# A recurrent scan beside a mixture of experts: VectorE's gate and GpSimd's expert product change places, the convolution leaves VectorE

## The chip, the core and the metric

The kernel runs on one core of a Trainium2 chip. The metric is the device time of one execution in microseconds. Five engines work beside one another, each through its own list of instructions in order: TensorE (PE in the rows; its weight loads are PEld), VectorE (DVE), ScalarE (ACT), GpSimd (POOL) and SyncE (SP), which only starts transfers. They wait for one another by semaphores alone.

## What is computed

For 4096 tokens of width 256, after a layer norm:

```
left, right = split(layernorm(xn) @ W_up + b_up)           # 128 + 128 channels
left  = silu(conv(left, 3 taps) + conv_b)                  # causal, per channel
delta = softplus(left @ W_delta + b_delta);  B, C = left @ W_B, left @ W_C
h[t]  = exp(delta[t] * A) * h[t-1] + delta[t] * left[t] * B[t]   # 128 channels x 64 states
y[t]  = sum over states of h[t] * C[t]  + left[t] * D
s     = xn + (y * silu(right)) @ W_down + b_down
g     = silu(sum over the 2 best of 8 experts of weight * (silu(xn @ w1) * (xn @ w3)) @ w2)
out   = x + s * g
```

## The kernel before

**The recurrence** has 128 x 64 rows of 4096 steps. Time is cut into 8 chunks of 512 steps, and each chunk into 64 *pairs* (two channels by 64 states on the 128 partitions), 512 pairs in all, numbered s. For each pair TensorE spreads delta*left over the partitions (`spread`, L1236), VectorE multiplies it by B (`mult`, L955), ScalarE forms exp(delta*A) (L733), VectorE scans (`scan`, L964), GpSimd multiplies by C (`state_by_c`, L433), and TensorE adds four pairs at a time into y (`reduce_quad`, L1170). The product of `mult` goes to a ring of two slots (B_RING), so `mult(s)` waits until `scan(s-2)` is through.

**The experts** are worked on between the pairs. There are 71 places for tiles of 128 rows, of which 67 are live with this data; from pair 16 on a tile takes 7 pairs, from tile 67 on 5. A tile has four steps, in its pairs 0, 2, 4 and 5: TensorE makes both products (L1222) in one of two banks, ScalarE takes tanh (L662, into th) and copies the other half (L664, into ue), VectorE gates (L976: th and the bank give gt), GpSimd multiplies gt by ue (`hidden`, L448), and TensorE applies w2 (`expert_out`, L1192) in pairs 3, 6, 8 and 8 of the tile. The rows of the next tile are transposed in pair 6 (L1205), and ScalarE evicts them (L654). A bank is taken again two turns later, and TensorE then waits for the gate that read it. The turns of a pair stand in `BY_PAIR[s]`.

**The order on each engine** is that of the loops over s, written by hand. TensorE in turn s issues `spread(s+1)`, a quad every fourth pair, and then the turns of pair s. VectorE: `mult(s)`, `scan(s-1)`, `gates` of pair s-1. GpSimd: `state_by_c(s-1)`, then `after_turns` of pair s-1 (`hidden`, or the gather of the next rows), then the scatter of results. ScalarE: the exp of pair s, then the work of the pair, then the evictions of pair s.

**The work for the next chunk** is spread over the pairs by a table, `WORK_AFTER`, with the number of parts in `WORK_PARTS`: the convolution on VectorE in pairs 14 to 16 of a chunk (L991 for the first tap, L994 for the two others), both tanhs on ScalarE in pair 17 (L600, L601), both sums with 1 in pair 18 (L606, L607), the two products on GpSimd in 19 and 20 (L475, L481), and later the softplus. Chunk 0 is prepared before the loop, its convolution on TensorE.

**The end**: after the pairs, the two results of each token are added (L542), passed through the silu, and mixed with x. The eight loads of x for this (L386, 512 KB each) are issued on SyncE's queue in one row in pair 12 of the last chunk, where the same queue also carries the expert weights and, for a tile that keeps its expert, the release of the next tile's weight slots (L350).

## Time and profile before

| | us |
|---|---|
| median of 3 runs (lowest, highest) | 1382.23 (1381.26, 1382.64) |
| the profiled execution: device time | 1385.34 |
| the profiled execution: its span | 1382.9 |

| engine | busy us | share of the span |
|---|---|---|
| TensorE | 1205.3 | 87% |
| VectorE | 1193.4 | 86% |
| GpSimd | 1089.5 | 79% |
| ScalarE | 734.1 | 53% |

The span goes from the first to the last instruction of the profiled execution; its device time holds 2.4 us more, and is 3.1 us above the median. The loop over pairs lies between about 113 and 1345 us, and the live expert tiles between about 183 and 1285 us. Where two starts on one engine are subtracted, the difference is called a pitch: VectorE starts an instruction before the last one has ended by its record, so that a pitch can be shorter than the duration.

### The profile page before, as it was taken

How to read it: one execution, taken by the hardware profiler on the slowest of the kernel's cores; microseconds unless marked ns; L12 is line 12 of the kernel's file. 1: busy time of each engine (PE TensorE's matmuls, PEld its weight loads, DVE VectorE, ACT ScalarE, POOL GpSimd, SP SyncE). 2: the span in 40 equal slices, each digit the busy share in tenths (PEclk: the TensorE clock that was granted, in tenths of full speed). 3: DMA queues.
4: the chain of work that ended last, by engine and by line, in shares of the span. 5: the costliest groups of instructions: out<-in, count | busy, mean ns of one | idle time of the engine just before them, and what ended most of it. 6: DMA issues, size and time to landing. Idle time of an engine off the chain costs nothing.

```text
span 1382.9 us, 26003 instructions
## 1 busy us (share of the span) xinstructions
PE 1205.3 (87%) x7688; PEld 938.9 (68%) x7688; DVE 1193.4 (86%) x1634; ACT 734.1 (53%) x1583; POOL 1089.5 (79%) x1048
## 2 busy tenths in 40 slices
PE   4846788999999999998899989998999999989761
PEld 4725366877677777876687768686777777877530
DVE  6747588999799998989798979898989988988988
ACT  1361556555655565546554565456545565545642
POOL 0346278898899788888998788788979788988994
PEclk8579999999999999999999999999999999999655
DMA  7111264646364645564556436643664457464458
GB/s 211 61 39 46 67 212 135 168 141 214 110 175 143 198 148 165 147 212 121 148 147 211 126 119 180 214 142 103 172 211 139 127 155 230 143 222 149 144 175 291
DMA packets 124316, 216.51 MB, mean 157 GB/s; under 512 B 15040, under 2 KB 40768, under 8 KB 124160
## 3 DMA queue, kind: packets, MB, share of 16 engines
q10 hardware_dynamic: 73728, 134.25, 33.9%
q1 hardware_dynamic: 43616, 61.83, 13.6%
q0 software_dynamic: 6816, 18.62, 4.2%
q8 instruction: 65, 1.06, 0.3%
q14 instruction: 91, 0.75, 0.2%
HBM read 190.67 MB, written 23.99 MB: 155 GB/s over the span
## 4 chain that ended last, share of the span: by engine, by line
PE 68%; POOL 9%; issue 8%; DVE 6%; DMA 4%; ACT 3%; SPq 1%; ACTq 0%; DVEq 0%; POOLq 0%
PE bank L1222 31%; PE bank L1192 14%; PE bank L1170 8%; PE bank L1236 6%; POOL arena L433 4%; DMA wring<-in_w_all 3%; PE bank L1099 2%; POOL hid L448 2%; DVE arena L964 2%; PE bank L1115 1%; PE bank L1135 1%; PE bank L1068 1%; PE bank L1061 1%; SPq L386 1%; PE bank L1205 1%
## 5 line engine op out<-in xcount | busy, mean ns | idle before, releaser
L433 POOL TENSOR_TENSOR arena<-arena,c_rep 128x512 f32<-128x512 f32 x512 | 607.1, 1190 | 153.4 <-DVE arena L964 145.6
L964 DVE TENSOR_TENSOR_SCAN arena<-bank,carry,arena 128x512 f32<-128x512 f32 x512 | 652.5, 1275 | 30.7 <-ACT bank L733 30.5
L1222 PEld LDWEIGHTS bank<-xgT,wring 128*128 128x128 f32 x4288 | 518.3, 194 | 138.4 <-issue 99.3
L1222 PE MATMUL bank<-xgT,wring 128*128 128x128 f32 x4288 | 540.6, 280 | 50.5 <-issue 26.4
L733 ACT ACTIVATE bank<-arena,a_neg 128x512 f32<-128x512 f32 x512 | 354.2, 692 | 107.7 <-ACT bank L733 43.2
L955 DVE TENSOR_TENSOR arena<-bank,b_rep 128x512 f32<-128x512 f32 x512 | 351.8, 687 | 42.6 <-PE bank L1236 23.4
L662 ACT ACTIVATE th<-bank 128x256 f32<-128x256 f32 x284 | 108.9, 383 | 347.0 <-PE bank L1222 324.9
L1236 PE MATMUL bank<-stack,pick 128*128 128x512 f32 x512 | 279.1, 546 | 8.3 <-DVE arena L955 7.9
L1192 PE MATMUL bank<-wring,hid 128*128 128x256 f32 x1072 | 271.4, 386 | 8.2 <-POOL hid L448 7.4
L1192 PEld LDWEIGHTS bank<-wring,hid 128*128 128x128 f32 x1072 | 196.1, 191 | 64.4 <-issue 24.6
L448 POOL TENSOR_TENSOR hid<-gt,ue 128x256 f32<-128x256 f32 x284 | 209.6, 738 | 15.4 <-DVE gt L976 11.8
L976 DVE SCALAR_TENSOR_TENSOR gt<-th,bank 128x256 f32<-128x256 f32 x284 | 114.9, 404 | 63.7 <-ACT th L662 47.9
L1170 PE MATMUL bank<-arena,win 128*32 128x512 f32 x1024 | 143.3, 633 | 7.7 <-POOL arena L433 7.6
L1236 PEld LDWEIGHTS bank<-stack,pick 128*128 128x128 f32 x512 | 101.5, 198 | 27.4 <-DVE arena L955 12.1
L664 ACT ACTIVATE ue<-bank 128x256 f32<-128x256 f32 x284 | 107.3, 378 | 0.0
L453 POOL DMA_INDIRECT results<-o_sb,dest x71 | 72.8, 1025 | 12.9 <-issue 12.3
L423 POOL DMA_INDIRECT xg<-xn_d,source x71 | 70.9, 998 | 10.7 <-issue 3.8
L1170 PEld LDWEIGHTS bank<-arena,win 128*32 128x32 f32 x1024 | 20.6, 110 | 50.9 <-issue 35.1
L407 POOL TENSOR_SCALAR pick<-hid,mask 128x2048 fp32r<-128x2048 f32 x2 | 10.9, 5468 | 45.6 <-DVE mask L813 45.6
L672 ACT ACTIVATE o_sb<-bank,weight 128x256 f32<-128x256 f32 x71 | 32.7, 460 | 10.1 <-PE bank L1192 10.1
L1061 PE MATMUL bank<-ident,xn 128*128 128x128 f32 x64 | 15.2, 421 | 18.4 <-DVE xn L804 18.4
L1157 PEld LDWEIGHTS bank<-ident 128*128 128x128 f32 x72 | 18.4, 310 | 18.7 <-issue 17.9
(172 smaller groups left out, 818.9 us busy)
## 6 DMA issues: line engine op xcount, KB each, us to landing
arena<-delta_d ACTq DMA_DIRECT2D x512, 256.0 KB
wring<-in_w_all SPq DMA_DIRECT2D x64, 384.0 KB, 5.6
xn<-in_x SPq DMA_DIRECT2D x4, 1024.0 KB, 9.9
xn_d<-xn SPq DMA_DIRECT2D x4, 1024.0 KB, 5.5
parts_d<-spare SPq DMA_DIRECT2D x16, 256.0 KB
stack<-parts_d SPq DMA_DIRECT2D x16, 256.0 KB, 5.7
wring<-results SPq DMA_DIRECT2D x8, 512.0 KB, 7.3
arena<-results SPq DMA_DIRECT2D x8, 512.0 KB, 7.9
```

What stands on the lines that cost most here:

```text
L433: pool.tensor_tensor(p_ring[:, s % P_RING, :], h_ring[:, s % H_RING, :], of_chunk(c_rep, c, 2), ALU.mult).then_inc(s_hc, 1)
L448: pool.tensor_tensor(hid[:, k % 4, :], gt[:, k % 2, :], ue[:, k % 2, :], ALU.mult).then_inc(s_hid, 1)
L662: act.activation(th[:, :], bank[:, 0:SW], ACT.Tanh, scale=0.5).then_inc(s_th, 1)
L664: act.activation(ue[:, k % 2, :], bank[:, SW:2 * SW], ACT.Copy).then_inc(s_ue, 1)
L733: act.activation(a_bank[s % 2][:, :], dl_ring[:, s % D_RING, :], ACT.Exp, scale=a_neg[:, s % PAIRS:s % PAIRS + 1]).then_inc(s_exp, 1)
L955: v.tensor_tensor(b_ring[:, s % B_RING, :], du_bank[s % 2][:, :], b_rep[:, cols(c)], ALU.mult).then_inc(s_bm, 1)
L964: v.tensor_tensor_scan(out=h_ring[:, s % H_RING, :], data0=a_bank[s % 2][:, :], data1=b_ring[:, s % B_RING, :], initial=carry[:, q:q + 1], ...
L976: v.scalar_tensor_tensor(out=gt[:, k % 2, :], in0=th[:, :], scalar=1.0, in1=bank_of((turn, i, j))[:, 0:SW], op0=ALU.add, op1=ALU.mult).the ...
L1170: ins = pe.matmul(y_bank[32 * g:32 * g + 32, :], win[:, 30 - 2 * i:62 - 2 * i], p_ring[:, (4 * q + g) % P_RING, :], start=False, stop=(i = ...
L1192: ins = pe.matmul(o_bank[:, 0:D], hid[:, k % 4, m * SLOT:(m + 1) * SLOT], wring[:, 2 * r + m, 4 * P:WROW], start=(r == 0 and m == 0), stop ...
L1222: ins = pe.matmul(bank[:, m * SW + r * SLOT:m * SW + (r + 1) * SLOT], wring[:, 2 * j + r, (2 * m + h) * P:(2 * m + h + 1) * P], xgT[:, i % ...
L1236: pe.matmul(du_bank[s % 2][:, :], pick[:, QUADS * (g % 2) + i16, :], stack[:, c % 2, g // 2, :], start=True, stop=True).then_inc(s_sel, 1)
```

## The change

VectorE's turn becomes `mult(s)`, `gates` of pair s-2, `scan(s-1)`. GpSimd's turn becomes `after_turns` of pair s-2, `state_by_c(s-1)`. The convolution is made by three ScalarE instructions (each tap's product, in pairs 10 to 12) and two GpSimd additions (pairs 12 and 13); the tanhs and the sums with 1 are taken one a pair, in pairs 15 to 18. The eight loads of x start in pair 10 of the last chunk, one every fifth pair.

VectorE, pairs 301 to 304, without other work between: L955 is the multiply, L964 the scan (its form is printed as SCALAR_TENSOR_TENSOR), L976 the gate.

```order
L955 TENSOR_TENSOR arena<-bank,b_rep 128x512
L964 SCALAR_TENSOR_TENSOR arena<-bank,carry,arena 128x512
L976 SCALAR_TENSOR_TENSOR gt<-th,bank 128x256
L955 TENSOR_TENSOR arena<-bank,b_rep 128x512
L964 SCALAR_TENSOR_TENSOR arena<-bank,carry,arena 128x512
L976 SCALAR_TENSOR_TENSOR gt<-th,bank 128x256
L955 TENSOR_TENSOR arena<-bank,b_rep 128x512
L964 SCALAR_TENSOR_TENSOR arena<-bank,carry,arena 128x512
L955 TENSOR_TENSOR arena<-bank,b_rep 128x512
```

The same place after; the multiply is L986 there, the scan L995 and the gate L1007.

```order
L986 TENSOR_TENSOR arena<-bank,b_rep 128x512
L995 SCALAR_TENSOR_TENSOR arena<-bank,carry,arena 128x512
L986 TENSOR_TENSOR arena<-bank,b_rep 128x512
L1007 SCALAR_TENSOR_TENSOR gt<-th,bank 128x256
L995 SCALAR_TENSOR_TENSOR arena<-bank,carry,arena 128x512
L986 TENSOR_TENSOR arena<-bank,b_rep 128x512
L1007 SCALAR_TENSOR_TENSOR gt<-th,bank 128x256
L995 SCALAR_TENSOR_TENSOR arena<-bank,carry,arena 128x512
L986 TENSOR_TENSOR arena<-bank,b_rep 128x512
L995 SCALAR_TENSOR_TENSOR arena<-bank,carry,arena 128x512
```

Both gates have moved from behind a scan to between a multiply and a scan, and every multiply now stands directly behind a scan.

VectorE, pairs 398 to 400, where the convolution of the last chunk stands (L991, L994; L1002 adds the output product).

```order
L955 TENSOR_TENSOR arena<-bank,b_rep 128x512
L964 SCALAR_TENSOR_TENSOR arena<-bank,carry,arena 128x512
L1002 TENSOR_TENSOR xn<-xn,bank 128x512
L991 TENSOR_SCALAR spare<-c_rep,half 128x512
L955 TENSOR_TENSOR arena<-bank,b_rep 128x512
L964 SCALAR_TENSOR_TENSOR arena<-bank,carry,arena 128x512
L976 SCALAR_TENSOR_TENSOR gt<-th,bank 128x256
L994 SCALAR_TENSOR_TENSOR spare<-c_rep,half,spare 128x512
L955 TENSOR_TENSOR arena<-bank,b_rep 128x512
L964 SCALAR_TENSOR_TENSOR arena<-bank,carry,arena 128x512
L976 SCALAR_TENSOR_TENSOR gt<-th,bank 128x256
L994 SCALAR_TENSOR_TENSOR spare<-c_rep,half,spare 128x512
```

The same place after.

```order
L986 TENSOR_TENSOR arena<-bank,b_rep 128x512
L1007 SCALAR_TENSOR_TENSOR gt<-th,bank 128x256
L995 SCALAR_TENSOR_TENSOR arena<-bank,carry,arena 128x512
L1021 TENSOR_TENSOR xn<-xn,bank 128x512
L986 TENSOR_TENSOR arena<-bank,b_rep 128x512
L995 SCALAR_TENSOR_TENSOR arena<-bank,carry,arena 128x512
L986 TENSOR_TENSOR arena<-bank,b_rep 128x512
L1007 SCALAR_TENSOR_TENSOR gt<-th,bank 128x256
L995 SCALAR_TENSOR_TENSOR arena<-bank,carry,arena 128x512
L986 TENSOR_TENSOR arena<-bank,b_rep 128x512
```

The three instructions of the convolution are gone from VectorE; nothing takes their place.

GpSimd in the pairs around 394: L433 is the product by C, L448 the expert product, L423 and L453 are the gather and the scatter.

```order
L448 TENSOR_TENSOR hid<-gt,ue 128x256
L433 TENSOR_TENSOR arena<-arena,c_rep 128x512
L423 DMA xg<-xn_d,source 128x256
L433 TENSOR_TENSOR arena<-arena,c_rep 128x512
L448 TENSOR_TENSOR hid<-gt,ue 128x256
L433 TENSOR_TENSOR arena<-arena,c_rep 128x512 x2
L448 TENSOR_TENSOR hid<-gt,ue 128x256
L453 DMA results<-o_sb,dest 17280x256
```

The same place after; L436 is the product by C, L451 the expert product, L478 the new addition.

```order
L451 TENSOR_TENSOR hid<-gt,ue 128x256
L436 TENSOR_TENSOR arena<-arena,c_rep 128x512
L426 DMA xg<-xn_d,source 128x256
L436 TENSOR_TENSOR arena<-arena,c_rep 128x512
L451 TENSOR_TENSOR hid<-gt,ue 128x256
L436 TENSOR_TENSOR arena<-arena,c_rep 128x512
L478 TENSOR_TENSOR spare<-spare 128x512
L436 TENSOR_TENSOR arena<-arena,c_rep 128x512
L456 DMA results<-o_sb,dest 17280x256
L478 TENSOR_TENSOR spare<-spare 128x512
L451 TENSOR_TENSOR hid<-gt,ue 128x256
```

The expert products stand ahead of the products by C of their turn, and two additions have come in.

```diff
-WORK_AFTER = dict(conv=("pairs", 14), tanh=("pairs", 17), sigmoid=("pairs", 18), silu=("pairs", 19), right=("pairs", 20),
+WORK_AFTER = dict(conv=("pairs", 10), add=("pairs", 12), tanh=("pairs", 15), sigmoid=("pairs", 17), silu=("pairs", 19),
...
+AGAIN_AT = (NC - 1) * PAIRS + 10
...
-                if s == (NC - 1) * PAIRS + 12:
+                if s == AGAIN_AT:
...
-                    for c in range(NC):
-                        sp.dma_start(x_again[c], x[0, cols(c), :].rearrange("(n p) c -> p n c", p=P)).then_inc(s_again, 16)
+                if s >= AGAIN_AT and (s - AGAIN_AT) % 5 == 0 and s < AGAIN_AT + 5 * NC:
+                    c = (s - AGAIN_AT) // 5
+                    sp.dma_start(x_again[c], x[0, cols(c), :].rearrange("(n p) c -> p n c", p=P)).then_inc(s_again, 16)
...
+            def add_taps(c, part):
+
+                pool.wait_ge(s_taps, 3 * (c - 1) + part + 2)
+                if part:
+                    pool.wait_ge(s_first_sum, c)
+                pool.tensor_tensor(stage("cv"), stage("cv"), stage(("thl", "thr")[part]), ALU.add
+                                   ).then_inc(s_cvs if part else s_first_sum, 1)
...
+                if s > 1:
+                    after_turns(BY_PAIR[s - 2])
                 if s:
                     state_by_c(s - 1)
-                    after_turns(BY_PAIR[s - 1])
...
+            def tap_product(c, part):
+
+                if part == 0:
+                    act.wait_ge(s_partd, STORES * c)
+                    act.wait_ge(s_lrev, c + 1)
+                tap = 2 - part
+                act.activation(stage(("cv", "thl", "thr")[part]), of_chunk(c_rep, c, tap), ACT.Identity,
+                               bias=0.0 if part else half[:, 3:4], scale=half[:, tap:tap + 1]).then_inc(s_taps, 1)
...
                 mult(s)
+                if s > 1:
+                    gates(BY_PAIR[s - 2])
                 if s:
                     scan(s - 1)
-                    gates(BY_PAIR[s - 1])
...
-                for name, t, r in WORK[s]:
-                    if name == "conv":
-                        conv(t, r)
+            gates(BY_PAIR[PAIR_COUNT - 2])
             scan(PAIR_COUNT - 1)
```

## Rows read from the trace of the kernel before

**Rows 1.** The page's first part: busy us, share of the span, instructions of an engine.

```profile
PE 1205.3 (87%) x7688; PEld 938.9 (68%) x7688; DVE 1193.4 (86%) x1634; ACT 734.1 (53%) x1583; POOL 1089.5 (79%) x1048
```

**Rows 2.** The timeline of pairs 302 to 304: start us, us, engine, line, operation.

```profile
854.18 0.69 DVE L955 TENSOR_TENSOR arena<-bank,b_rep 128x512 f32<-128x512 f32 x1
...
854.78 1.28 DVE L964 TENSOR_TENSOR_SCAN arena<-bank,carry,arena 128x512 f32<-128x512 f32 x1
...
854.94 0.35 PEld L1205 LDWEIGHTS bank<-ident,xg 128*128 128x128 f32 x2
...
855.12 0.38 ACT L662 ACTIVATE th<-bank 128x256 f32<-128x256 f32 x1 [0.57 <-PE bank L1222]
...
855.75 0.69 ACT L733 ACTIVATE bank<-arena,a_neg 128x512 f32<-128x512 f32 x1
855.98 0.40 DVE L976 SCALAR_TENSOR_TENSOR gt<-th,bank 128x256 f32<-128x256 f32 x1
...
856.14 1.09 POOL L433 TENSOR_TENSOR arena<-arena,c_rep 128x512 f32<-128x512 f32 x1 [0.42 <-DVE arena L964]
856.29 0.69 DVE L955 TENSOR_TENSOR arena<-bank,b_rep 128x512 f32<-128x512 f32 x1
...
856.89 1.27 DVE L964 TENSOR_TENSOR_SCAN arena<-bank,carry,arena 128x512 f32<-128x512 f32 x1
...
857.19 0.73 POOL L448 TENSOR_TENSOR hid<-gt,ue 128x256 f32<-128x256 f32 x1
857.55 1.86 PEld L1222 LDWEIGHTS bank<-xgT,wring 128*128 128x128 f32 x16 [0.84 <-issue]
...
858.27 0.69 DVE L955 TENSOR_TENSOR arena<-bank,b_rep 128x512 f32<-128x512 f32 x1
```

**Rows 3.** VectorE's busy time in the seven pairs from 296 on, by stretch.

```profile
841.64:856.29 14.65, 14.27 (x20) 1.00 0.60 169
```

**Rows 4.** The timeline: VectorE's multiplies of pairs 16 and 485.

```profile
184.24 0.68 DVE L955 TENSOR_TENSOR arena<-bank,b_rep 128x512 f32<-128x512 f32 x1
...
1284.62 0.68 DVE L955 TENSOR_TENSOR arena<-bank,b_rep 128x512 f32<-128x512 f32 x1
```

**Rows 5.** The page's costliest groups: count, busy us, mean ns, idle us before and releasers.

```profile
L976 DVE SCALAR_TENSOR_TENSOR gt<-th,bank 128x256 f32<-128x256 f32 x284 | 114.9, 404 | 63.7 <-ACT th L662 47.9
```

**Rows 6.** Groups by line: the convolution, one GpSimd product and one ScalarE sum.

```profile
L994 DVE SCALAR_TENSOR_TENSOR spare<-c_rep,half,spare 128x512 f32<-128x512 f32 x14 | 19.2, 1374 | 0.0
...
L475 POOL TENSOR_TENSOR spare<-spare 128x512 f32<-128x512 f32 x8 | 10.2, 1275 | 20.7 <-ACT spare L607 20.7
...
L991 DVE TENSOR_SCALAR spare<-c_rep,half 128x512 f32<-128x512 f32 x7 | 8.1, 1157 | 0.0
...
L607 ACT ACTIVATE spare<-spare 128x512 f32<-128x512 f32 x8 | 4.9, 617 | 0.0
```

**Rows 7.** The timeline behind the convolution's second instruction in pair 399.

```profile
1086.83 1.48 DVE L994 SCALAR_TENSOR_TENSOR spare<-c_rep,half,spare 128x512 f32<-128x512 f32 x1
...
1088.23 0.68 DVE L955 TENSOR_TENSOR arena<-bank,b_rep 128x512 f32<-128x512 f32 x1
...
1090.46 1.86 PEld L1222 LDWEIGHTS bank<-xgT,wring 128*128 128x128 f32 x16 [1.32 <-DVE gt L976]
```

**Rows 8.** The timeline in pair 464: SyncE's last load of x, TensorE's next step.

```profile
1237.05 4.49 SPq L386 DMA_DIRECT2D c_rep<-in_x  x1
...
1242.12 2.71 PE L1222 MATMUL bank<-xgT,wring 128*128 128x128 f32 x16 [4.00 <-SPq L350]
```

**Rows 9.** The timeline late in the loop: two multiplies with a gate between.

```profile
1321.43 0.69 DVE L955 TENSOR_TENSOR arena<-bank,b_rep 128x512 f32<-128x512 f32 x1
...
1323.54 0.69 DVE L955 TENSOR_TENSOR arena<-bank,b_rep 128x512 f32<-128x512 f32 x1
```

More of the change, by code:

```diff
@@ L42 @@
 LOAD_OF = dict(step=4, out=2, rows=1, down=2, delta=2, b=2, c=2)
-WORK_AFTER = dict(conv=("pairs", 14), tanh=("pairs", 17), sigmoid=("pairs", 18), silu=("pairs", 19), right=("pairs", 20),
+WORK_AFTER = dict(conv=("pairs", 10), add=("pairs", 12), tanh=("pairs", 15), sigmoid=("pairs", 17), silu=("pairs", 19),
+                  right=("pairs", 20),
                   exp=("delta", 2), ln=("delta", 3),
@@ L47 @@
                   stack=("delta", 17))
-WORK_PARTS = dict(sum=4, conv=3)
+WORK_PARTS = dict(sum=4, conv=3, add=2, tanh=2, sigmoid=2)
 BIAS_AT = 61
+AGAIN_AT = (NC - 1) * PAIRS + 10
 def turns_by_pair():
@@ L264, in mamba_and_experts @@
         s_val, s_hot, s_perm, s_placed = (sem(k) for k in ("s_val", "s_hot", "s_perm", "s_placed"))
-        s_cv, s_cvs, s_taps, s_tanh, s_sig, s_u, s_sr = (sem(k) for k in ("s_cv", "s_cvs", "s_taps", "s_tanh", "s_sig", "s_u", "s_sr"))
+        s_cv, s_cvs, s_taps, s_first_sum, s_tanh, s_sig, s_u, s_sr = (sem(k) for k in ("s_cv", "s_cvs", "s_taps", "s_first_sum", "s_tanh", "s_sig", "s_u", "s_sr"))
         s_dp, s_bc, s_bcev, s_sp, s_dlt, s_hi = (sem(k) for k in ("s_dp", "s_bc", "s_bcev", "s_sp", "s_dlt", "s_hi"))
@@ L477, in gate_of_right @@
             def gate_of_right(c):
-                pool.wait_ge(s_sig, c + 1)
+                pool.wait_ge(s_sig, 2 * c + 2)
                 ge(pool, s_dn, 2 * (c - 1))
@@ L525, in _ @@
                 for name, c, r in WORK[s]:
-                    if name == "silu":
+                    if name == "add":
+                        add_taps(c, r)
+                    elif name == "silu":
                         silu_of_left(c)
@@ L535, in _ @@
                     bias_rows(s // PAIRS)
+            for here in BY_PAIR[PAIR_COUNT - 2:PAIR_COUNT]:
+                after_turns(here)
             state_by_c(PAIR_COUNT - 1)
@@ L595, in evict_conv, with tanhs, sigmoids @@
                 act.activation(stage("cv"), product_bank(c, "conv")[:, :], ACT.Identity, bias=half[:, 3:4]).then_inc(s_cvs, 1)
-            def tanhs(c):
-                act.wait_ge(s_cvs, c + 1)
-                act.activation(stage("thl"), stage("cv"), ACT.Tanh)
-                act.activation(stage("thr"), b_rep[:, cols(c)], ACT.Tanh).then_inc(s_tanh, 1)
-            def sigmoids(c):
-                act.wait_ge(s_tanh, c + 1)
-                act.activation(stage("thl"), stage("thl"), ACT.Identity, bias=1.0)
-                act.activation(stage("thr"), stage("thr"), ACT.Identity, bias=1.0).then_inc(s_sig, 1)
+            def tap_product(c, part):
[5 more added lines that the diff above has]
+                               bias=0.0 if part else half[:, 3:4], scale=half[:, tap:tap + 1]).then_inc(s_taps, 1)
+            def tanhs(c, part):
+                if part == 0:
+                    act.wait_ge(s_cvs, c + 1)
+                    act.activation(stage("thl"), stage("cv"), ACT.Tanh).then_inc(s_tanh, 1)
+                else:
+                    act.activation(stage("thr"), b_rep[:, cols(c)], ACT.Tanh).then_inc(s_tanh, 1)
+            def sigmoids(c, part):
+                act.wait_ge(s_tanh, 2 * c + 1 + part)
+                name = ("thl", "thr")[part]
+                act.activation(stage(name), stage(name), ACT.Identity, bias=1.0).then_inc(s_sig, 1)
             def softplus(c, part):
@@ L706, in _ @@
             evict_conv(0)
-            tanhs(0)
-            sigmoids(0)
+            for part in range(2):
+                tanhs(0, part)
+            for part in range(2):
+                sigmoids(0, part)
             scale_rows(3)
@@ L739, in _ @@
                 for name, c, r in WORK[s]:
-                    if name == "tanh":
-                        tanhs(c)
+                    if name == "conv":
+                        tap_product(c, r)
+                    elif name == "tanh":
+                        tanhs(c, r)
                     elif name == "sigmoid":
-                        sigmoids(c)
+                        sigmoids(c, r)
                     elif name in ("exp", "ln", "less"):
@@ L983, in gate_chunk @@
                 v.tensor_tensor(sr[:, c % 2, :], y_bank[:, :], sr[:, c % 2, :], ALU.mult).then_inc(s_gated, 1)
-            def conv(c, tap):
-                cv = stage("cv")
-                if tap == 0:
-                    v.wait_ge(s_partd, STORES * c)
-                    v.wait_ge(s_lrev, c + 1)
-                    v.tensor_scalar(cv, of_chunk(c_rep, c, 2), half[:, 2:3], half[:, 3:4], ALU.mult, ALU.add).then_inc(s_taps, 1)
-                else:
-                    v.wait_ge(s_taps, 2 * (c - 1) + tap)
-                    v.scalar_tensor_tensor(out=cv, in0=of_chunk(c_rep, c, 2 - tap), scalar=half[:, 2 - tap:3 - tap],
-                                           in1=cv, op0=ALU.mult, op1=ALU.add).then_inc(s_taps if tap == 1 else s_cvs, 1)
             def add_rows(c, h):
```

2 lines of the change are left out of this document (1 added, 1 removed).

## The prediction, made before the changed kernel had run

> **What bounds the kernel now.** I read the page's first part first: TensorE is busy for 87% of the span, VectorE for 86% and GpSimd for 79% [rows 1]. None of these says which engine sets the pace, so I went to the timeline of a stretch in which nothing but scans and expert steps runs. There VectorE alternates between three things, and the reader should look at the pitches (start to start), not at the durations. With a gate behind the scan a pair takes 0.60 (multiply to scan, 854.18 to 854.78) + 1.20 (scan to gate) + 0.31 (gate to the next multiply) = 2.11 us; without one, 0.60 + 1.38 (scan at 856.89, multiply at 858.27) = 1.98 us [rows 2]. A gate that lasts 0.40 us by its record thus costs 0.13 us: most of it lies in a gap that is there without it, since a multiply waits for the scan two pairs back, which is the scan just issued, and the gate needs nothing of that scan. A tile of seven pairs with four gates is 4 x 2.11 + 3 x 1.98 = 14.38 us of VectorE at the least. The seven pairs from 296 on took 14.65 us [rows 3], and TensorE has its own work packed closely there too. So the two engines are almost level, VectorE with 0.3 to 0.5 us to spare in a tile.
>
> Over the whole, the 67 live tiles take from 184.24 to 1284.62 us by the multiplies of pairs 16 and 485, 1100.4 us or 16.4 us each [rows 4]. The 2.0 us above 14.4 are stalls of few kinds: new expert weights, the softplus on ScalarE, the convolution, and one long stall near 1240 us. After that come the pairs from 485 on, whose experts are mostly dead, at VectorE's pace, and a mixing stage that the change leaves alone.
>
> **The gate between multiply and scan.** What it removes is a wait: before 284 gates VectorE sat idle for 63.7 us, 47.9 of it for tanh [rows 5]. With one more pair between TensorE's step and the gate this wait should be nearly gone. I give little for it, because it is not lost time of VectorE's alone: the scan behind the gate needs the exp of its pair, and ScalarE makes that after the same tanh and copy (855.12, then 855.75) [rows 2]. In a stalled pair the scan comes hardly earlier, whichever side of it the gate is on.
>
> What it adds is the gap. Now every multiply stands behind a scan and waits it out: 0.60 (multiply to gate, taken as multiply to scan) + 0.31 (gate to what follows) + 1.38 = 2.29 us for a pair with a gate, against 2.11: +0.18 us. No row has a gate in that place; the pitch behind a multiply could only be seen with a scan. The bounds of the price are 0 and 0.31 us, the gate's whole pitch; I take 0.18, since all its parts are pitches of these two kinds. A tile then needs 4 x 2.29 + 3 x 1.98 = 15.10 us of VectorE, 0.72 more, and that is above what TensorE needs, so in quiet stretches VectorE becomes the bound. I laid 15.10 us (plus what other VectorE work a tile has) against each of the 67 tiles, from the multiplies of every seventh pair (the first and the last stand in the rows) [rows 4]. Of 59 tiles without a convolution 20 were shorter, by 8.2 us together. The other 39 have idle time of over 0.72 us, which takes most of it up; I charge 0.1 us each, 4 us (bounds 0 and 0.72 each, 28 us). The 8 tiles with a convolution were full, so they pay 0.72 each, 5.8 us. **Together +18 us**, bounds 0 and 67 x 0.72 = 48.
>
> The Trainium skill speaks against this term: VectorE: DVE Perf Modes, section "The DRAIN you can't avoid", has the next operation wait until the pipe is empty whether or not there is a semaphore, so that "the semaphore costs nothing extra here". By that rule the order of the three instructions costs nothing and the term is 0. The trace differs by 0.18 us between scan to gate and scan to multiply [rows 2], and I go by the trace.
>
> The gate also comes later, behind `mult` of two pairs on: about 0.6 + 0.4 + 0.1 = 1.1 us behind the start of that multiply. TensorE takes the banks back in pairs 6 and 0 of a tile: with multiplies at 854.18 and 856.29 the gates would be through at 855.3 and 857.4, where it began the transposes at 854.94 and the step at 857.55 [rows 2]. The first is 0.3 us late, the second just in time, and the step waits on ScalarE's eviction of the rows anyway. This is inside the 15.10 us pace, so no term of its own.
>
> **GpSimd's order.** Before, the expert product started 1.05 us behind the product by C (856.14, 857.19), which had waited for the scan [rows 2]. After, it needs the gate alone, which ends as the scan starts, and fits under the 1.27 us of the scan. The gate comes some 0.7 us later than now and the product follows at once, so hid is ready at about the same time: 0 us, with GpSimd less pressed. The gather goes one pair later, with some five pairs to land: 0. Nothing is late by it: what is queued behind the expert product's wait is the product by C, which could not start before the scan's end, and the only waiter on that is a quad four pairs on.
>
> **The convolution.** Off VectorE: 7 of L991 and 14 of L994, 8.1 + 19.2 = 27.3 us [rows 6]. It was all on the path: the multiply that follows starts only 1.40 us behind the second instruction (1086.83, 1088.23), and TensorE then waited 1.32 us for a gate (1090.46) [rows 7]. With it gone the tiles cannot fall to VectorE's floor everywhere: +1.4 us for other stalls, 0.2 a tile. On ScalarE 21 new instructions of about 0.62 us each (taken from L607 [rows 6]), one a pair; tanhs and sums keep their number but no longer come two at a time. ScalarE is idle for half the time, but the eviction of rows stands behind this work in three pairs of seven: 7 chunks x 3/7 x 0.62 = 1.9 us. On GpSimd 14 additions of about 1.28 us (as L475 [rows 6]), hidden by its 21% of idle time, save where a tile's third and fourth expert product is waited for: +1 us, bounds 0 and 5. The convolution also loses its wait of ScalarE for VectorE, which I leave at 0. **Together -27.3 + 1.4 + 1.9 + 1.0 = -23 us**, bounds -27 and -15.
>
> **The loads of x.** In one row they filled the queue: the last took 4.49 us to issue from 1237.05, and TensorE waited 4.00 us, until 1242.12, for SyncE's release of a weight slot (L350), which had to stand behind them [rows 8]. By the multiplies of every seventh pair that tile lasted 21.0 us, its neighbours 15.5 and 15.0. With one load every fifth pair, about 11 us apart, the queue should stay free. The first is issued two pairs earlier, when the buffers' last readers are through; no later one waits for anything new. **-5.3 us**, bounds -4 and -6.
>
> **The end.** In the last pairs VectorE goes at 2.11 us a pair with a gate (1321.43, 1323.54) [rows 9]: that is the VectorE-bound pace. 16 gates of dead tiles x 0.18 = 2.9 us; a wait for tanh in the first of them goes and GpSimd, which ends the loop, was behind VectorE by more than an addition: **+2 us**, bounds 0 and 3.
>
> **The sum** is 18 - 23 - 5.3 + 2 = -8.3 us. Against the profiled execution this is a span of 1382.9 - 8.3 = 1374.6 us and a device time of 1377; its time stands 3.1 us above the median, and from the median it is 1382.2 - 8.2 = **1374 us**.
>
> **The rivals.**
> *The gap is free.* If an instruction without a wait in front of the scan, or a gate that no longer waits for tanh, is worth 0.18 us a time after all, the terms of 18 and 2 go: 1382 - 28 = 1354 us. For it: the 63.7 us of idle time before gates [rows 5], and that a gap with a semaphore is only 0.18 us long. Against: the same gap in every pair without a gate [rows 2]. Chance 0.20. (The Trainium skill's rule of "The DRAIN you can't avoid", VectorE: DVE Perf Modes, would have it so; the trace does not agree.)
> *The gap is paid in every tile* (the slower one). If TensorE's late banks in pairs 6 and 0 add to VectorE's loss, so that a stall elsewhere no longer takes it up, all 67 tiles pay 0.72 us: +48 + 3 - 28 = +23, 1405 us. It decides from about 0.4 us a tile on, where the 27 us outweigh the 28 saved. For it: the transposes would be 0.3 us late already at VectorE's present position. Against: 39 of the 59 tiles without convolution hold stalls in which VectorE catches up. Chance 0.20.
> *The work moved costs what it saved.* ScalarE's eviction of rows is waited for in nearly every tile, and each delay of it reaches TensorE; with GpSimd late too, the convolution brings -10 instead of -23: 1387 us. Chance 0.13.
> *The loads of x bring nothing*, since the queue blocks wherever a load stands: 1379.5 us. Chance 0.05.
>
> **How the numbers follow.** The forecast has 0.42; alone it spans 1367 to 1381. The range reaches towards both far rivals, 1357 to 1393, and leaves out the ends of either. About 0.2% (2.8 us) is what a measurement of this kernel can tell from no change, so faster means below 1379.4 and slower above 1385.0. Faster: 0.36 of the forecast, 0.20 and 0.03 of the last two: 0.59. Slower: 0.19, 0.08 and 0.01: 0.28. The same: 0.13.
>
> **What the profile after would show.** The pitch of multiply to gate to scan to multiply is the first thing: 0.60, 0.31 and 1.38 confirm the price; a scan to multiply of 1.2 refutes it. Idle time before the gate should fall from 63.7 to under 10 us. Quiet tiles should take 15.1 us, not 14.7, and the seven tiles with a later chunk's convolution about 16 instead of 18.3. TensorE's idle time for gates grows, that for SyncE near 1240 us is gone. I am wrong if the loop's gain is over 25 us, if tiles stay at 14.7, or if the eviction of rows on ScalarE comes later over the whole chunk.

## The result, and the profile of the changed kernel

The changed kernel takes 1390.42 us (median of 14 runs, 1385.45 to 1395.42), the kernel before 1383.42 us beside it (1379.24 to 1388.08). The ratio is 1.0049, 95% interval 1.0032 to 1.0066: slower by 7 us, where 8 us faster was forecast. The profiled execution of the changed kernel took 1393.09 us, 2.7 above its median.

The page's first part and five of its groups, as in [rows 1, 5]: busy us, mean ns, idle us before and what ended it.

```profile
PE 1210.9 (87%) x7688; PEld 940.3 (68%) x7688; DVE 1193.6 (86%) x1613; ACT 747.4 (54%) x1604; POOL 1103.5 (79%) x1062
...
L986 DVE TENSOR_TENSOR arena<-bank,b_rep 128x512 f32<-128x512 f32 x512 | 354.1, 692 | 107.0 <-PE bank L1254 62.0
...
L689 ACT ACTIVATE th<-bank 128x256 f32<-128x256 f32 x284 | 108.9, 384 | 355.8 <-PE bank L1240 310.2
...
L451 POOL TENSOR_TENSOR hid<-gt,ue 128x256 f32<-128x256 f32 x284 | 208.0, 733 | 15.7 <-DVE gt L1007 13.2
...
L1007 DVE SCALAR_TENSOR_TENSOR gt<-th,bank 128x256 f32<-128x256 f32 x284 | 116.6, 411 | 0.1
```

The wait before the gate is gone, 63.7 us to 0.1 [rows 5], and VectorE has 21 instructions less, yet it is busy for the same 1193.6 us. The idle time now stands before the multiply, 107.0 us (42.6 before). Of these 107.0 us, 62.0 (23.4 before) are 68 waits for TensorE's spread: stalls that VectorE had met at the gate it now meets at the multiply. Another 44.1 us (18.7 before) are 418 gaps of about 0.1 us each, and their rise is what the new order itself adds. VectorE's timeline in a stretch with nothing but scans and steps, as in [rows 2], shows where they come from:

```profile
854.85 0.41 DVE L1007 SCALAR_TENSOR_TENSOR gt<-th,bank 128x256 f32<-128x256 f32 x1
855.18 1.28 DVE L995 TENSOR_TENSOR_SCAN arena<-bank,carry,arena 128x512 f32<-128x512 f32 x1
856.56 0.69 DVE L986 TENSOR_TENSOR arena<-bank,b_rep 128x512 f32<-128x512 f32 x1
857.17 1.27 DVE L995 TENSOR_TENSOR_SCAN arena<-bank,carry,arena 128x512 f32<-128x512 f32 x1
858.55 0.69 DVE L986 TENSOR_TENSOR arena<-bank,b_rep 128x512 f32<-128x512 f32 x1
859.15 0.41 DVE L1007 SCALAR_TENSOR_TENSOR gt<-th,bank 128x256 f32<-128x256 f32 x1
859.48 1.28 DVE L995 TENSOR_TENSOR_SCAN arena<-bank,carry,arena 128x512 f32<-128x512 f32 x1
860.86 0.69 DVE L986 TENSOR_TENSOR arena<-bank,b_rep 128x512 f32<-128x512 f32 x1
```

A pair with a gate goes at 0.60 + 0.33 + 1.38 = 2.31 us (858.55 to 860.86), one without at 1.99. Between 200 and 1290 us there are 386 places where a multiply stands behind a scan and waits for nothing else; before there were 162, and most of the other scans had a gate behind them. Quiet tiles, which took 14.37 us at their shortest, now take 15.23, and ten take exactly that.

The waits between 200 and 1290 us (waiter, what ended the wait, us in total, times, longest) show what the later gate does to others:

```profile
PEld bank L1240 <- DVE gt L1007: 47.4, 55, 1.6
...
ACT th L689 <- DVE gt L1007: 28.7, 28, 1.8
...
PEld bank L1223 <- DVE gt L1007: 14.4, 24, 1.0
```

TensorE now waits for gates (in the same stretch before: 28.6 us of weight loads of the step, 3.4 of the transposes), as an engine does that is no longer the pace.

### The profile page after: what moved, and what is told of

It is laid out like the page before. It is cut to its first block, busy times and chain, and to the rows that moved or that the text cites. A ratio compares the mean times of both kernels' runs of the same rounds, so it can differ in the third digit from the quotient of the medians.

```text
span 1391.3 us, 26024 instructions
## 1 busy us (share of the span) xinstructions
PE 1210.9 (87%) x7688; PEld 940.3 (68%) x7688; DVE 1193.6 (86%) x1613; ACT 747.4 (54%) x1604; POOL 1103.5 (79%) x1062
## 4 chain that ended last, share of the span: by engine, by line
PE 52%; DVE 13%; issue 11%; POOL 11%; DMA 5%; ACT 5%; SPq 1%; DVEq 1%; ACTq 1%; POOLq 0%
PE bank L1240 22%; PE bank L1210 10%; DVE arena L995 8%; PE bank L1188 6%; POOL arena L436 5%; PE bank L1254 4%; DMA wring<-in_w_all 3%; DVE gt L1007 2%; PE bank L1117 2%; POOL hid L451 2%; ACT bank L762 2%; PE bank L1079 1%; PE bank L1153 1%; PE bank L1086 1%; PE bank L1133 1%
## 5 line engine op out<-in xcount | busy, mean ns | idle before, releaser
L436 POOL TENSOR_TENSOR arena<-arena,c_rep 128x512 f32<-128x512 f32 x512 | 604.5, 1184 | 147.4 <-DVE arena L995 136.0
L995 DVE TENSOR_TENSOR_SCAN arena<-bank,carry,arena 128x512 f32<-128x512 f32 x512 | 653.8, 1277 | 38.6 <-ACT bank L762 33.0
L986 DVE TENSOR_TENSOR arena<-bank,b_rep 128x512 f32<-128x512 f32 x512 | 354.1, 692 | 107.0 <-PE bank L1254 62.0
L451 POOL TENSOR_TENSOR hid<-gt,ue 128x256 f32<-128x256 f32 x284 | 208.0, 733 | 15.7 <-DVE gt L1007 13.2
L1007 DVE SCALAR_TENSOR_TENSOR gt<-th,bank 128x256 f32<-128x256 f32 x284 | 116.6, 411 | 0.1
L1223 PEld LDWEIGHTS bank<-ident,xg 128*128 128x128 f32 x134 | 15.9, 141 | 28.9 <-DVE gt L1007 15.6
```

The costliest lines, as they stand in the source:

```text
L436: pool.tensor_tensor(p_ring[:, s % P_RING, :], h_ring[:, s % H_RING, :], of_chunk(c_rep, c, 2), ALU.mult).then_inc(s_hc, 1)
L451: pool.tensor_tensor(hid[:, k % 4, :], gt[:, k % 2, :], ue[:, k % 2, :], ALU.mult).then_inc(s_hid, 1)
L986: v.tensor_tensor(b_ring[:, s % B_RING, :], du_bank[s % 2][:, :], b_rep[:, cols(c)], ALU.mult).then_inc(s_bm, 1)
L995: v.tensor_tensor_scan(out=h_ring[:, s % H_RING, :], data0=a_bank[s % 2][:, :], data1=b_ring[:, s % B_RING, :], initial=carry[:, q:q + 1], ...
L1007: v.scalar_tensor_tensor(out=gt[:, k % 2, :], in0=th[:, :], scalar=1.0, in1=bank_of((turn, i, j))[:, 0:SW], op0=ALU.add, op1=ALU.mult).the ...
```

## The experiments

Two questions stood open: what the two orders cost and why, and why the convolution and the loads of x together did not outweigh them. Each kernel was timed beside the kernel before, whose medians were 1383.59, 1384.21 and 1383.81 us in the three batches. A difference in us is worked out from the ratio and its 95% interval; the difference of the two medians can be up to 2 us off it. The line numbers move a little between the kernels. In the diffs "before" and "after" are the two kernels of the case.

**The parts one by one.** The two orders alone, in the kernel before:

```diff
                 mult(s)
+                if s > 1:
+                    gates(BY_PAIR[s - 2])
                 if s:
                     scan(s - 1)
-                    gates(BY_PAIR[s - 1])
...
+                if s > 1:
+                    after_turns(BY_PAIR[s - 2])
                 if s:
                     state_by_c(s - 1)
-                    after_turns(BY_PAIR[s - 1])
```

> The kernel before with the two orders alone (VectorE's gate between multiply and scan, GpSimd's expert product and gather ahead of its product by C, both a pair later); convolution and loads of x as before. Theory A (the orders cost what the whole change lost and also what the rest brought): +25 to +35 us over the kernel before, about 1413 us, with 15.23 us in every quiet tile. Theory B (the moved convolution brings little, so the orders cost little more than the 7 us of the whole change): +8 to +14 us, about 1394 us. Theory C (the orders help and the other parts did the harm): below 1383 us.

1400.74 us, ratio 1.0130 [1.0101, 1.0159]: +18 us (+14 to +22), between theories A and B, and close to the 18 + 2 of the prediction's terms. But this sum hides two parts of opposite sign. By the tiles of its profile, the 17 quiet tiles (those under 15.10 us before) grew by 11.3 us together and 41 others by 3.9 (the one at pair 464 left out); the eight tiles with a convolution became 5.1 us *shorter* (5.4 and 5.9 against two other executions with the old order of VectorE). The convolution's own instructions on VectorE fell from 27.3 to 17.4 us, although nothing in them was changed. The timelines show what goes with it. In the old order a gate or another instruction often stood between the scan and an instruction of the convolution, and GpSimd's product, which waits for the same scan, started first:

```profile
1086.67 1.09 POOL L433 TENSOR_TENSOR arena<-arena,c_rep 128x512 f32<-128x512 f32 x1 [2.16 <-DVE arena L964]
1086.83 1.48 DVE L994 SCALAR_TENSOR_TENSOR spare<-c_rep,half,spare 128x512 f32<-128x512 f32 x1
```

With the orders changed no gate stands there, and the instruction of the convolution (L997 there) starts first:

```profile
1093.95 0.72 DVE L997 SCALAR_TENSOR_TENSOR spare<-c_rep,half,spare 128x512 f32<-128x512 f32 x1
1094.11 1.52 POOL L433 TENSOR_TENSOR arena<-arena,c_rep 128x512 f32<-128x512 f32 x1 [2.16 <-DVE arena L967]
```

In the kernel before 13 of the 21 instructions are long (1.14 to 2.79 us), with the new orders 3, and all 16 long ones start while GpSimd is at a product or a gather. Of the 26 short ones (0.52 to 0.73 us) five do too: three beside a gather, two in the last 0.1 us of a product. No run tested this by itself.

The spread loads alone, in the kernel before:

```diff
+AGAIN_AT = (NC - 1) * PAIRS + 10
...
-                if s == (NC - 1) * PAIRS + 12:
+                if s == AGAIN_AT:
...
-                    for c in range(NC):
-                        sp.dma_start(x_again[c], x[0, cols(c), :].rearrange("(n p) c -> p n c", p=P)).then_inc(s_again, 16)
+                if s >= AGAIN_AT and (s - AGAIN_AT) % 5 == 0 and s < AGAIN_AT + 5 * NC:
+                    c = (s - AGAIN_AT) // 5
+                    sp.dma_start(x_again[c], x[0, cols(c), :].rearrange("(n p) c -> p n c", p=P)).then_inc(s_again, 16)
```

> The kernel before with the eight loads of x spread, one every fifth pair, and nothing else. Theory A: the stall near 1240 us goes, -4 to -6 us, about 1378 us. Theory B: the loads now meet the gathers of the short tiles (three pairs apart), which land later, and give the gain back: within 2 us of the kernel before.

1383.17 us, ratio 0.9984 [0.9966, 1.0003]: -2.2 us (-4.7 to +0.4), not told from nothing (the medians differ by 0.4). The stall that the loads had made is gone: the tile at pair 464 lasts 15.12 us instead of 20.98 (15.61 in the changed kernel). But 20.98 us was a long one: in the five other profiles with the loads in a row, of kernels further below, that tile takes 17.2 to 19.4 us, and TensorE waits 1.9 to 3.1 us for SyncE there, not 4.0. Over all six the tile takes 18.9 us in the mean, 3.8 more than with spread loads. And from pair 485 on the loop takes 2.2 us more (57.2 instead of 55.0); where is shown below.

The changed kernel with both orders put back (the first diff in reverse), so the convolution and the loads:

> The changed kernel with both orders put back (gate behind the scan, expert product behind the product by C), so the convolution off VectorE and the spread loads alone. Theory A: -20 to -28 us against the kernel before, about 1359 us, the fastest so far. Theory B (ScalarE and GpSimd give most of it back): -5 to -10 us, about 1376 us. Theory C: slower than the kernel before.

1370.61 us, ratio 0.9895 [0.9865, 0.9925]: -14.5 us (-18.7 to -10.4), between theories A and B. And the same with the loads of x in a row again, so the convolution alone:

> As the run before it, but the loads of x in one row as in the kernel before: the convolution's move alone. Theory A: -15 to -22 us, about 1364 us. Theory B: -2 to -6 us. Its difference to the run before is the price of the loads' row a second time, -4 to -6 us by theory A.

1373.04 us, ratio 0.9922 [0.9898, 0.9946]: -10.8 us (-14.1 to -7.5), in neither theory's range, and half of the 23 forecast.

The tiles say where the other half is. Lengths of the tiles beside a convolution, by the multiplies of every seventh pair:

| tile from pair | 16 | 72 | 79 | 142 | 205 | 268 | 331 | 394 |
|---|---|---|---|---|---|---|---|---|
| before, us | 14.82 | 16.45 | 17.91 | 17.91 | 19.28 | 17.56 | 19.35 | 19.39 |
| convolution alone moved | 14.73 | 15.12 | 17.61 | 18.64 | 16.13 | 15.13 | 15.92 | 16.14 |
| convolution and loads moved | 14.60 | 15.11 | 19.41 | 18.63 | 16.14 | 15.12 | 15.92 | 16.13 |
| changed kernel | 15.34 | 15.61 | 17.67 | 17.84 | 16.75 | 15.78 | 15.94 | 15.76 |

The last four of the seven convolutions gained 2.4 to 3.4 us each; the second (pairs 78 to 80, in two tiles) 1.6, the third (tile from 142) -0.7. The 1.6 does not repeat: with the loads moved too, the tile from 79 takes 19.41 us and the gain is gone, while the third and the last four come out the same. The first convolution stands in pairs 14 to 16, where the live tiles begin. From the multiply of pair 10 to that of 23 the kernel before takes 36.36 us and this one 36.18, so it gained 0.2. Two things are different there in the kernel before. The three instructions last only 1.98 us together (3.24 to 4.95 in the other chunks), and before the multiplies and scans from pair 13 to 18 VectorE sits idle for 3.85 us, 2.1 of it in one wait for TensorE's spread and 1.0 in one for ScalarE's exp. The busy times in the tiles from 142 and 331 (us from:to, length, then busy us of TensorE, its weight loads, VectorE, ScalarE and GpSimd, granted clock, DMA share, GB/s), before:

```profile
473.18:491.09 17.91, 16.31 (x111) 12.52 (x109) 17.91 (x24) 10.39 (x24) 13.51 (x14) 1.00 0.72 252
920.74:940.09 19.35, 16.60 (x111) 12.70 (x109) 18.90 (x23) 10.00 (x24) 14.31 (x14) 1.00 0.44 125
```

and with the convolution alone moved:

```profile
468.89:487.52 18.63, 16.32 (x111) 12.51 (x109) 14.86 (x20) 10.38 (x24) 16.05 (x17) 1.00 0.81 244
907.16:923.08 15.92, 15.72 (x111) 12.61 (x109) 14.77 (x21) 11.43 (x24) 15.45 (x15) 1.00 0.41 132
```

In both tiles VectorE lost 3 to 4 us of work. The second became 3.4 us shorter, the first no shorter at all. Its transfers differ: 244 to 252 GB/s against 125 to 132, since new expert weights come in there. TensorE's step waited for them already in the kernel before, beside the convolution:

```profile
477.51 2.43 DVE L994 SCALAR_TENSOR_TENSOR spare<-c_rep,half,spare 128x512 f32<-128x512 f32 x1
479.72 2.02 PE L1222 MATMUL bank<-xgT,wring 128*128 128x128 f32 x16 [0.49 <-DMA wring<-in_w_all]
```

and with the convolution alone moved the same wait is still there and longer, 2.0 us in the tile instead of 1.3 (L1233 is the step there):

```profile
475.35 2.02 PE L1233 MATMUL bank<-xgT,wring 128*128 128x128 f32 x16 [0.41 <-DMA wring<-in_w_all]
477.41 0.38 ACT L684 ACTIVATE th<-bank 128x256 f32<-128x256 f32 x1 [2.19 <-PE bank L1233]
...
478.16 0.42 DVE L1002 SCALAR_TENSOR_TENSOR gt<-th,bank 128x256 f32<-128x256 f32 x1 [1.30 <-ACT th L684]
...
481.16 2.02 PE L1233 MATMUL bank<-xgT,wring 128*128 128x128 f32 x16 [1.60 <-DMA wring<-in_w_all]
...
483.22 0.39 ACT L684 ACTIVATE th<-bank 128x256 f32<-128x256 f32 x1 [2.59 <-PE bank L1233]
...
483.97 0.42 DVE L1002 SCALAR_TENSOR_TENSOR gt<-th,bank 128x256 f32<-128x256 f32 x1 [1.23 <-ACT th L684]
```

A slot of weights lands, TensorE starts its step at 481.16, the tanh follows at 483.22 and the gate at 483.97, after VectorE has stood idle for 1.23 us. In this tile VectorE now waits 3.5 us for tanhs, where it made the convolution before. That the transfers set the tile's length is read from these waits; no run took them away. Over the live tiles its waits for a tanh grew from 46.6 us in the kernel before to:

```profile
DVE gt L1002 <- ACT th L684: 60.6, 66, 3.2
```

**Where the orders' price comes from.** Two buffers for `th`, so that a tanh need not wait for the gate before it. In the changed kernel the tanh of a tile's last step starts within 0.2 us of that gate's end 29 times, before 9 times.

```diff
-                ge(act, s_gt, k)
-                act.activation(th[:, :], bank[:, 0:SW], ACT.Tanh, scale=0.5).then_inc(s_th, 1)
+                ge(act, s_gt, k - 1)
+                act.activation(th[:, k % 2, :], bank[:, 0:SW], ACT.Tanh, scale=0.5).then_inc(s_th, 1)
...
-                        v.scalar_tensor_tensor(out=gt[:, k % 2, :], in0=th[:, :], scalar=1.0,
+                        v.scalar_tensor_tensor(out=gt[:, k % 2, :], in0=th[:, k % 2, :], scalar=1.0,
```

> The changed kernel with two buffers for tanh instead of one, so that tanh of a step no longer waits for the gate of the step before it (in the changed kernel ScalarE waits 41.3 us for gates there, 12.0 before). Theory A (VectorE's own pace bounds the quiet tiles, tanh's wait lies beside it): -1 to -4 us, about 1388 us, quiet tiles still 15.2 us. Theory B (the late gate hurts by stopping ScalarE): -8 us or more, below 1383 us.

1391.73 us, ratio 1.0045 [1.0021, 1.0070]: as the changed kernel, so neither theory's gain came. The wait falls from 28.7 us (above) to 0.4 and the time stays: it cost nothing.

The gather put back a pair earlier, in the changed kernel:

```diff
+            def gathers(here):
...
+                for turn, i, k in here:
+                    if turn == "rows" and i + 1 < TILES:
+                        gather_rows(i + 1)
...
                     state_by_c(s - 1)
+                    gathers(BY_PAIR[s - 1])
```

> The changed kernel with only the gather of the next rows put back one pair earlier, behind the product by C. Theory A: in the short tiles at the end rows come every five pairs and TensorE waits for the gather, so the pairs from 485 to 511 fall from 61.4 to about 58 us and the whole by 3 us; nothing before pair 485 moves. Theory B: the gather is hidden, and it stays at 1390 us.

1392.99 us, ratio 1.0062 [1.0041, 1.0084]: as the changed kernel. The gather's place is not the cause, and the stall of pair 488 stays (3.53 us instead of 3.70).

A third slot in `b_ring`, so that a multiply no longer waits for the scan just ahead of it. To make room, the ring of GpSimd's products (P_RING) has seven slots instead of eight, here and in the three kernels below that have the third slot:

```diff
-H_RING, P_RING, B_RING, D_RING = 8, 8, 2, 4
+H_RING, P_RING, B_RING, D_RING = 8, 7, 3, 4
```

> The changed kernel with three slots for the multiply's products instead of two (and seven instead of eight for the products by C), so that no multiply waits for the scan just ahead of it. Theory A (the price of the gate's new place is that wait of 0.18 to 0.2 us behind every scan): scan to multiply falls from 1.38 to 1.19 us, VectorE's floor of a tile from 15.25 to 13.9 us, quiet tiles to 14.6 to 14.9 us (TensorE's pace), and the time by 12 to 22 us, to about 1373 us. Theory B (the bank that comes back late is what bounds): pitch falls, but quiet tiles stay at 15.2 us and the time at 1388 us.

1368.33 us, ratio 0.9889 [0.9852, 0.9926]: 22 us off the changed kernel, by one slot. Its VectorE in a quiet stretch:

```profile
844.61 1.28 DVE L995 TENSOR_TENSOR_SCAN arena<-bank,carry,arena 128x512 f32<-128x512 f32 x1
845.81 0.67 DVE L986 TENSOR_TENSOR arena<-bank,b_rep 128x512 f32<-128x512 f32 x1
846.39 0.41 DVE L1007 SCALAR_TENSOR_TENSOR gt<-th,bank 128x256 f32<-128x256 f32 x1
846.72 1.28 DVE L995 TENSOR_TENSOR_SCAN arena<-bank,carry,arena 128x512 f32<-128x512 f32 x1
847.91 0.67 DVE L986 TENSOR_TENSOR arena<-bank,b_rep 128x512 f32<-128x512 f32 x1
```

Scan to multiply is 1.19 to 1.20 us (846.72 to 847.91), not 1.38, and the pair with a gate takes 2.10. The order of the instructions is the changed kernel's; only what the multiply waits for differs. The same slot with the old orders, the convolution and the loads moved:

> The kernel with the convolution off VectorE, spread loads and the old orders (median 1370.6 us), with three slots for the multiply's products and seven for the products by C. Theory A: VectorE's floor of a tile falls from 14.37 to 13.8 us, below TensorE's pace, so it saves what VectorE had bound: -3 to -8 us, about 1365 us. Theory B: TensorE and ScalarE set everything already, within 2 us of 1370.6.

1370.69 us, ratio 0.9904 [0.9872, 0.9935]; and the slot alone in the kernel before:

> The kernel before with three slots for the multiply's products and seven for the products by C, and nothing else. Theory A (with the gate behind the scan most of the wait is already used, so a third slot brings only what VectorE bound in the convolution's tiles and a few full tiles): -2 to -6 us, about 1379 us. Theory B (the third slot is a gain of its own, whatever the order, and its 22 us in the changed kernel say nothing about the order): -12 us or more, below 1372 us.

1383.78 us, ratio 0.9990 [0.9965, 1.0015]. In the old order the slot is worth nothing (1370.61 without, 1370.69 with it; 1383.81 and 1383.78). There a gate already stands in four of a tile's seven gaps; that TensorE's work leaves VectorE no use for the others is the likely reason, not shown. So the two orders cost 18 to 21 us with two slots (the first experiment, and 1.0049 against 0.9895 by the ratios) and nothing with three (1368.33 against 1370.69): the self-wait behind the scan is their whole price. Nor do they gain anything clear of the noise with three slots, although the 63.7 us of idle time before the gate is gone: in that kernel VectorE waits 85.2 us for TensorE's spread before the multiply (27.4 with the old orders and three slots), so the stalls moved there, as above.

**GpSimd's half.** The gate moved, but GpSimd's expert product and gather one pair later and still behind the product by C:

```diff
                 if s:
                     state_by_c(s - 1)
-                    after_turns(BY_PAIR[s - 1])
+                if s > 1:
+                    after_turns(BY_PAIR[s - 2])
```

> The kernel before with VectorE's gate moved between multiply and scan; GpSimd's expert product and gather go one pair later with it but stay behind the product by C. Theory A (the price is VectorE's): +15 to +19 us, as with both orders (ratio 1.013). Theory B (GpSimd's order matters, and expert products behind the product by C come too late for TensorE): +22 us or more.

1436.27 us, ratio 1.0381 [1.0334, 1.0428]: +53 us, more than either theory gave. TensorE's second product of a step in its page:

```profile
L1197 PE MATMUL bank<-wring,hid 128*128 128x256 f32 x1072 | 279.9, 391 | 44.1 <-POOL hid L448 43.6
...
L1197 PEld LDWEIGHTS bank<-wring,hid 128*128 128x128 f32 x1072 | 189.1, 190 | 114.8 <-POOL hid L448 88.1
```

A gate that stands ahead of a scan, with an expert product that stands behind the product of that same scan, gives 2.96 us from the gate's start to the product's at the median and 2.73 at the least, against 1.12 and 0.49 in the changed kernel, and TensorE waits for hid. GpSimd's new order is what the gate's move needs; the kernel with both orders is 36 us faster (1400.74). Alone, in the kernel before (the second half of the first diff):

> The kernel before with GpSimd's order alone changed: expert product and gather of pair s-2 ahead of the product by C of pair s-1; VectorE as before. Theory A (the expert product is needed late, and its place is free): within 2 us of the kernel before. Theory B (a part of the price is GpSimd's): +4 us or more.

1385.42 us, ratio 1.0010 [0.9982, 1.0037]: nothing, as the prediction had it (in the old order of VectorE).

**The end.** From the multiply of pair 485 to that of 511 the kernel before takes 55.0 us, the changed one 61.4. (In executions of other kernels with the old order and the old loads it is 54.2 to 56.3.) 16 gates at 2.32 instead of 2.11 us are 3.4 of it. Another 2.8 us are one stall in pair 488 (5.9 us to the next multiply instead of 3.1), in the changed kernel's timeline:

```profile
1288.98 0.99 POOL L426 DMA_INDIRECT xg<-xn_d,source  x1
1289.23 0.37 SPq L389 DMA_DIRECT2D b_rep<-in_x  x1
...
1296.07 1.07 PE L1175 MATMUL bank<-ident 128*128 128x2 f32 x4 [5.57 <-issue]
...
1297.81 0.69 DVE L986 TENSOR_TENSOR arena<-bank,b_rep 128x512 f32<-128x512 f32 x1 [3.70 <-PE bank L1254]
```

The gather of the next rows is issued at 1288.98 and the next work on TensorE starts at 1296.07, 7.1 us later; a load of x stands 0.25 us behind the gather. With GpSimd's order alone and the loads in a row, there is no load beside it and it is 4.5 us:

```profile
1282.18 0.99 POOL L423 DMA_INDIRECT xg<-xn_d,source  x1
...
1286.68 0.77 PE L1160 MATMUL bank<-ident 128*128 128x2 f32 x4 [3.07 <-issue]
```

With the spread loads alone it is 6.0 (1286.04 to 1292.06). To move the load out of the way, one every second pair, with three slots, two `th` and the old orders:

```diff
-                if s >= AGAIN_AT and (s - AGAIN_AT) % 5 == 0 and s < AGAIN_AT + 5 * NC:
-                    c = (s - AGAIN_AT) // 5
+                if s >= AGAIN_AT and (s - AGAIN_AT) % 2 == 0 and s < AGAIN_AT + 2 * NC:
+                    c = (s - AGAIN_AT) // 2
```

> Old orders, convolution off VectorE, three slots for the multiply's products, two for tanh, and the loads of x one every second pair from pair 458, so that the last is issued in pair 472, ahead of the short tiles. Theory A (a load of x in pair 488 delayed the gather of the rows and cost 3 us there): -2 to -4 us against the 1370.7 us of the same with every fifth pair, about 1368 us, with 2.7 to 3.1 us between the multiplies of pairs 488 and 489 instead of 5.3 to 5.9. Theory B (loads two pairs apart block the queue again near 1240 us): 1370 to 1374 us.

1367.89 us, ratio 0.9890 [0.9846, 0.9934], as fast as any, and not told from the 1370.69 us of the same with every fifth pair and one `th`. Its end takes 55.3 us, but its gather still takes 5.6 (1266.72 to 1272.30), and pair 488 takes 4.9 us without a load beside, where theory A had 2.7 to 3.1. In seven profiles with a load right behind the gather that time is 5.75 to 7.1 us, in the seven without one 3.8 to 5.6. So the load is likely a part of the delay, but not all of it: that kernel with the load in pair 488 has 5.75 us and this one 5.6. What makes up the rest is open.

Five kernels beat both: the changed kernel with a third slot (1368.33), the convolution's move alone (1373.04), and the convolution and loads with the old orders, alone (1370.61), with a third slot (1370.69), and with the loads closer (1367.89). Their intervals overlap; they are 0.8 to 1.1% ahead of the kernel before.

## Why the prediction was wrong

| term | forecast, us | measured, us |
|---|---|---|
| both orders (18 + 2) | +20 | +18 (+14 to +22) |
| convolution | -23 | -10.8 (-14.1 to -7.5) |
| loads of x | -5.3 | -2.2 (-4.7 to +0.4) |
| sum | -8.3 | +5.0; the whole changed kernel +7 |

The forecast lost its sign in the two gains. The price of the orders came out right as a sum, in part by luck. The measured parts leave 2 us of the whole unexplained, within their intervals. They need not add up, either: the new orders alone shorten the convolution's instructions on VectorE from 27.3 to 17.4 us, so that there was less to save in the changed kernel than the 27.3 us that my sum starts from.

**The gate between multiply and scan: right in cause and pitch, lucky in the sum.** 2.29 us a gated pair was forecast and 2.31 is there, 15.10 a quiet tile and 15.23 is there; the 0.33 us from gate to scan (0.31 taken) is most of the difference. But of my 18 us, 5.8 were for the eight tiles with a convolution, which "were full", and these became 5.1 us shorter with the orders alone, where most of the convolution's instructions now start ahead of GpSimd's products. The quiet tiles cost more than I gave them, 11.3 us for 8.2, the others 3.9 us, as given. By the tiles that is 10 us, and the end adds 3. These two profiled executions are 13.1 us apart, the timed runs 18 us, and I can't say in which tiles the rest lies. Of the idle time before the gate I had counted nothing as gain, and the third slot bears that out: with the gap gone, the new order is as fast as the old. The gap-is-free rival falls with the pitch of 1.38. The Trainium skill's rule behind it (VectorE: DVE Perf Modes, "The DRAIN you can't avoid") was measured there on equal copies, and the section adds that a next operation that is not held starts earlier. For the scan and the multiply "the semaphore costs nothing extra" does not hold: 1.38 us with a wait on the scan, 1.20 without one, in the same order. The rival in which every tile pays 0.72 us (+51 for both orders) falls too: the 41 other tiles paid 0.1 us each.

**The convolution: the step that failed.** "It was all on the path" was read from one place, the chunk around pair 399 [rows 7], and multiplied by seven. That chunk and three more did gain: 12.3 us of the 16.8 us that their instructions lasted, and the +1.4, +1.9 and +1.0 of my sum had allowed for the 4.5 us between. The other three brought 0.2, 1.6 and -0.7 of their 10.6 us, and this is the miss, 9.5 us. At two of them (tiles from 79 and 142) new expert weights come in and TensorE's step waits for them, with the convolution on VectorE or off it. At the first, VectorE waited for TensorE and ScalarE, and the instructions lasted 1.98 us, not 3.9. By the tiles that is a gain of 13.4 us, by the timed runs 10.8; the 1.6 us of the second, which did not repeat, are within that difference. My bounds of -27 and -15 took only GpSimd's and ScalarE's cost into account, and no chunk with another cover. ScalarE's taps took 0.74 us each where 0.62 was taken (21 instructions, so 2.5 us more busy time), and GpSimd's additions 1.28 as taken. I had the rival "the work moved costs what it saved" with -10 for this term, and its size came true, but not its reason: TensorE's waits for hid between 200 and 1290 us are 24.6 us with the convolution moved and 25.3 before. Beside new weights, what was saved became VectorE's wait for a tanh, behind TensorE and its weights.

**The loads of x: mis-sized.** The stall went as forecast, 20.98 to 15.12 us with the loads alone. But the -5.3 was read from one execution, whose stall was the longest of six; their mean gives 3.8 us. I also left out that a spread load can meet the gather of pair 488: the end took 2.2 us longer with the loads alone. 3.8 less 2.2 is 1.6, and the timed runs have 2.2.

**The gather, a pair later: 0, right.** Put back, nothing changed. **GpSimd's order: 0, right** alone, though I had not seen that the gate's move without it would cost 53 us.

**The end: +2 forecast, +6.4 in the profile**: 3.4 of the gates (2.9 taken), and 2.8 of pair 488.

**Late banks.** Missed: the one buffer of `th`, which the later gate holds longer. Two buffers brought nothing.

**What the profile was to show.** The pitches 0.60, 0.31 and 1.38: yes, with 0.33 for the second. Idle time before the gate under 10 us: 0.1. Quiet tiles at 15.1: 15.23. Convolution tiles at about 16: the later four yes (15.76 to 16.75), those beside new weights no (17.67, 17.84). The stall near 1240 gone: yes.

A caution on stage sums: from the multiply of pair 16 to that of 485 the kernel before took 1100.4 us in its profile and the changed kernel 1100.7, but two kernels that are no faster in the timed runs (third slot alone, GpSimd's order alone) took 1091.4 and 1094.1. A stage's length from one execution scatters by some 9 us, so the terms in the table are from timed runs. Pitches repeat, and most tiles do. The tiles beside new weights and beside the row of loads do not: with the convolution moved and the old orders the tile from 79 took 17.6, 19.4, 19.8 and 20.3 us in four kernels.

## What to carry to other kernels

A small instruction behind a long one that its successor must wait for anyway is nearly free; before moving it, give the successor another buffer, or the gap opens. Here one slot made 22 us of difference in one order and nothing in the other, so slots and order are to be tried together. A part of a change can also change the price of another part: here an order of two engines took 10 us off a convolution that it did not touch. A saving that was read at one place counts only at the repetitions where nothing else ends last: look at each (here seven), above all at those with a transfer beside. And taking work out of an order that is paced elsewhere should be tested alone: two thirds of this change were a gain of 1%, hidden by the third.

## What was not expected of the hardware

A multiply that waits for the scan directly ahead of it starts 1.38 us behind the scan's start, one that waits for an older scan 1.20 us, less than the scan's own 1.28. This 0.18 us, at 224 more places than before (40 us), lengthened the kernel by 18 to 21 us. A convolution instruction of VectorE that was recorded at 0.72 us where it started 0.16 us ahead of GpSimd's product was recorded at 1.48 us where it started 0.16 us behind one. A gather's rows were used 4.5 us after its issue in one kernel, and 7.1 us after it where a load of x was issued 0.25 us behind it from another engine's queue.
